# Splitting a kernel's first loads by need and over two queues, with the first projections ahead of the folded weights

## The reference, cut to what matters

```python
k = conv1x1(xA, wk, bk)         # all three: 256 channels -> 128, n = 1024 places
v = conv1x1(xA, wv, bv)
q = conv1x1(xA, wq, bq)
attn = softmax(einsum('bcn,bcm->bnm', v, q), axis=2)
av   = einsum('bcn,bnm->bcm', k, attn)
avw  = einsum('oc,bcn->bon', wwg, av)
avw  = (avw - bn1_m) * bn1_g / sqrt(bn1_v + eps) + bn1_b
o    = conv1x1(avw, wout, bout)
o    = (o - bn2_m) * bn2_g / sqrt(bn2_v + eps) + bn2_b
x    = relu(o + xA)
# then, per image: t = t + attention(layernorm(t)); t = t + experts(layernorm(t))
```

## Time and profile before

| | us |
|---|---|
| median of 3 runs | 1248.38 |
| lowest and highest | 1245.92, 1252.49 |
| the profiled execution | 1251.72 |
| its span, first to last instruction | 1249.9 |
| PE busy in it | 1120.8 (90%) |
| DVE busy | 794.2 (64%) |
| ACT busy | 634.3 (51%) |
| POOL busy | 577.8 (46%) |

### The profile page before, as it was taken

One profiled execution on the slowest core, in us unless ns is written; L12 is line 12 of the kernel. 1 busy time (PEld: TensorE's weight loads), 2 busy tenths in 40 slices (PEclk: granted clock), 3 DMA queues, 4 the chain that ended last, 5 costly groups with the idle time before them and its releaser, 6 DMA issues.

```text
span 1249.9 us, 28738 instructions
## 1 busy us (share of the span) xinstructions
PE 1120.8 (90%) x10344; PEld 739.8 (59%) x10344; DVE 794.2 (64%) x1458; ACT 634.3 (51%) x1147; POOL 577.8 (46%) x461
## 2 busy tenths in 40 slices
PE   3999999975799999899989998689899999999993
PEld 1555555533344554454445444578799989998772
DVE  2666666655788888678768872666566555555540
ACT  0757575742477668666765675433233333333432
POOL 2425242413488761675276337256454444454420
PEclk9999999977799999999999999799999999999996
DMA  5235852544022230333243214623333233332228
GB/s 164 63 114 185 317 187 80 186 130 146 27 74 78 83 78 27 96 95 95 63 109 88 57 45 127 251 36 71 51 50 47 47 49 51 53 52 40 41 31 273
DMA packets 98854, 120.50 MB, mean 96 GB/s; under 512 B 29120, under 2 KB 76032, under 8 KB 98080
## 3 DMA queue, kind: packets, MB, share of 16 engines
q1 hardware_dynamic: 77744, 70.15, 19.0%
q0 software_dynamic: 20544, 42.22, 15.2%
q10 hardware_dynamic: 432, 6.29, 1.3%
HBM read 72.84 MB, written 45.60 MB: 95 GB/s over the span
## 4 chain that ended last, share of the span: by engine, by line
PE 80%; DVE 5%; DMA 4%; ACT 3%; issue 3%; SPq 1%; DVEq 1%; another core or an unknown queue 0%; POOL 0%; ACTq 0%; POOLq 0%
PE PP L945 25%; PE PP L1313 14%; PE PP L1201 9%; PE PP L1175 9%; PE PP L1029 4%; PE PP L1080 4%; PE PP L1126 3%; PE PP L1185 3%; PE PP L1190 2%; DVE mxp L1539 2%; PE PP L977 2%; DMA WB<-late_d 2%; ACT WB L872 1%; PE PP L1054 1%; PE PP L1280 1%
## 5 line engine op out<-in xcount | busy, mean ns | idle before, releaser
L872 ACT ACTIVATE WB<-PP 128x512 f32<-128x512 f32 x512 | 268.4, 604 | 174.8 <-PE PP L1201 174.8
L1539 DVE TENSOR_REDUCE mxp<-PP 128x2 f32<-128x1024 f32 x256 | 301.3, 1219 | 66.0 <-PE PP L1126 64.4
L916 ACT ACTIVATE WORK<-PP,b1c 128x256 f32<-128x256 f32 (+1 forms) x320 | 142.4, 450 | 266.0 <-PE PP L945 248.5
L945 PE MATMUL PP<-WORK,WB 128*128 128x256 f16 (+2 forms) x1984 | 221.1, 268 | 18.1 <-issue 9.7
L672 POOL TENSOR_TENSOR WB<-WB 128x1024 f32<-128x1024 f32 x80 | 188.9, 2361 | 78.2 <-PE PP L1190 69.4
L945 PEld LDWEIGHTS PP<-WORK,WB 128*128 (+1 forms) x1984 | 186.1, 103 | 49.2 <-issue 21.4
L728 POOL DMA_INDIRECT res_d<-WORK,lb x71 | 116.1, 1635 | 200.1 <-DVE WORK L1779 180.2
L1313 PE MATMUL PP<-WB,WORK 128*128 x1704 | 194.9, 273 | 0.0
L1313 PEld LDWEIGHTS PP<-WB,WORK 128*128 128x128 f16 x1704 | 164.4, 98 | 22.0 <-issue 0.9
L1201 PE MATMUL PP<-WORK 97*128 97x256 f16 x1024 | 159.3, 279 | 16.0 <-ACT WB L872 12.9
L638 POOL TENSOR_TENSOR WB<-WORK,WB 128x1024 f16<-128x1024 f32 x32 | 68.4, 2137 | 174.0 <-ACT WORK L778 173.9
(11 more groups left out here) (287 smaller groups left out, 1144.0 us busy)
## 6 DMA issues: line engine op xcount, KB each, us to landing
WORK<-in_L_ffn_W_dram POOLq DMA_DIRECT2D x32, 512.0 KB, 4.3
res_d<-WORK SPq DMA_DIRECT2D x8, 1024.0 KB, 4.5
late_d<-WB POOLq DMA_DIRECT2D x1, 6144.0 KB, 19.1
WB<-late_d ACTq DMA_DIRECT2D x3, 2048.0 KB, 14.8
v_d<-WORK SPq DMA_DIRECT2D x4, 1024.0 KB, 4.5
WORK<-q_hi_d SPq DMA_DIRECT2D x16, 256.0 KB, 3.6
WORK<-v_d SPq DMA_DIRECT2D x8, 512.0 KB, 5.8
WORK<-k_hi_d SPq DMA_DIRECT2D x16, 256.0 KB, 3.9
```

What stands on the lines that cost most here:

```text
L872: act.activation(PR[n % 3][:, c // 2, c % 2 * 2:c % 2 * 2 + 2], SCORES[m % 3] .rearrange("p (h n) -> p h n", h=2), ACT.Exp).then_inc(s("e_ ...
L916: act.activation(hid[:, k, 0:width], hidden_bank(k)[:, 0:width], ACT.Gelu, bias=b1c[:, bass.ds(e, 1), k], scale=1.0 / WSCALE)\
L945: mm = pe.matmul(dst, lhsT, rhs, start=(n == 0), stop=(n == len(pairs) - 1))
L1539: dve.tensor_reduce(mxp[:, n // 4 % 2, i, h:h + 2, k], PP[2 + h // 2][:, :].rearrange("p (h n) -> p h n", h=2), X_AXIS, ALU.max).then_inc( ...
```

## The change

The list of 28 loads is taken apart. SyncE issues `wq` and `wv` first, on a semaphore of their own (`ld_qv`), then the first image, then the other seven weights on `ld_w`, and raises the 27 semaphores of `PLACES` only then. The vectors go to ScalarE's queue, at the head of its program, as 13 loads on `ld_vec`: where a vector has 256 values, one load fills two columns of `vec`, where there were two loads. TensorE transposes `wq` and `wv` as soon as these two are there, each into the PSUM tile that has no other use then, and VectorE copies them one by one (`wqv_kept`). TensorE projects q, waits for the seven weights, transposes the remaining ones, projects v, computes the folded weights, and projects k. `dve_prep` counts three steps now: the constants' input (1), the copies of the remaining transposes (2), the folded weights (3). Nothing is computed otherwise than before.

```diff
-LOADS = 28
+LOADS = 7
+VECTORS = 13
@@ sync
-            for name in PLACES.split():
-                sp.sem_inc(s(name), FREE)
+            sp.dma_start(wq_raw, wq).then_inc(s("ld_qv"), 16)
+            sp.dma_start(wv_raw, wv).then_inc(s("ld_qv"), 16)
+            load_x(0)
             n_w = 0
-            for dst, src in ((wq_raw, wq), (wv_raw, wv), (wk_raw, wk),
+            for dst, src in ((wk_raw, wk),
                              (wo_raw, wout.rearrange("(c p) i -> p c i", p=P)), (wwg_raw, wwg),
...
-                             (vec[:, BQ:BQ + 1], col(bq)), (vec[:, BV:BV + 1], col(bv)),
...
+            for name in PLACES.split():
+                sp.sem_inc(s(name), FREE)
...
-            load_x(0)
             load_x(1)
@@ scalar
+            for at, src in ((BQ, bq), (BV, bv), (BK, bk), (G1, bn1_g), (BB1, bn1_b), (M1, bn1_m), (V1, bn1_v),
+                            (BO, bout), (G2, bn2_g), (BB2, bn2_b), (M2, bn2_m), (V2, bn2_v), (BA, b_out)):
+                n = src.shape[0] // P
+                act.dma_start(vec[:, at:at + n], src.rearrange("(c p) -> p c", p=P), allow_slow_non_contiguous=True).then_inc(s("ld_vec"), 16)
             act.wait_ge(s("dve_prep"), 1)
             act.activation(vec[:, 24:27], vec[:, 24:27], ACT.Sqrt).then_inc(s("act_prep"), 1)
-            act.wait_ge(s("dve_prep"), 2)
+            act.wait_ge(s("ld_vec"), 16 * VECTORS)
@@ tensor
             pe.wait_ge(s("pool_const"), 1)
-            pe.wait_ge(s("ld_w"), 16 * LOADS)
...
+            pe.wait_ge(s("ld_qv"), 32)
+            for i, raw in enumerate((wq_raw, wv_raw)):
+                for c in range(CC):
+                    mm = pe.transpose(PP[3 - i][:, 2 * i * C + c * P:2 * i * C + (c + 1) * P],
+                                      raw[:, c * P:(c + 1) * P], identf[:, :])
+                mm.then_inc(s("pe_prep"), 1)
...
+            pe.wait_ge(s("wqv_kept"), 1)
             for c in range(CC):
                 project_q(0, c)
+            pe.wait_ge(s("ld_w"), 16 * LOADS)
+            for c in range(CC):
+                pe.transpose(PP[2][:, c * P:(c + 1) * P], wo_raw[:, c], identf[:, :])
+            pe.transpose(PP[2][:, 384:384 + E * HC], b1_raw, identf[0:E * HC, 0:E * HC])
+            pe.transpose(PP[2][:, 256:384], wwg_raw, identf[:, :]).then_inc(s("pe_prep"), 1)
+            pe.wait_ge(s("wqv_kept"), 2)
             project_v(0)
+            pe.wait_ge(s("dve_prep"), 2)
+            for c in range(CC):
+                product(PP[3][:, 512 + c * P:512 + (c + 1) * P], [(wk_raw[:, c * P:(c + 1) * P], wwgT)])
+            pe.wait_ge(s("ones_kept"), 1)
+            product(PP[3][:, 896:896 + E], [(ones_all, wr_raw[:, c]) for c in range(CC)])
+            product(PP[3][:, 768:896], [(bkr, wwgT)], "pe_prep")
+            pe.wait_ge(s("dve_prep"), 3)
             project_k(0)
@@ vector
-            dve.wait_ge(s("ld_w"), 16 * LOADS)
...
+            for i, dst in enumerate((wqT, wvT)):
+                dve.wait_ge(s("pe_prep"), i + 1)
+                dve.tensor_copy(dst, PP[3 - i][:, 2 * i * C:(2 * i + 1) * C].rearrange("p (c n) -> p c n", c=CC))\
+                   .then_inc(s("wqv_kept"), 1)
+            dve.wait_ge(s("ld_vec"), 16 * VECTORS)
...
+            dve.sem_inc(s("dve_prep"), 1)
+            dve.wait_ge(s("pe_prep"), 3)
+            dve.tensor_copy(woT, PP[2][:, 0:256].rearrange("p (c n) -> p c n", c=CC))
+            dve.tensor_copy(wwgT, PP[2][:, 256:384])
+            dve.tensor_copy(b1c[:, :, :], PP[2][:, 384:384 + E * HC].rearrange("p (e k) -> p e k", e=E))
```

More of the change, by code:

```diff
@@ L325, in s @@
             return S[name]
-        for name in ("q_low v_low ld_w ld_x0 ld_x1 ld_y0 ld_y1 bst_kept pool_const pe_prep dve_prep act_prep "
+        for name in ("ld_qv ld_vec wqv_kept q_low v_low ld_w ld_x0 ld_x1 ld_y0 ld_y1 bst_kept pool_const pe_prep dve_prep act_prep "
                      "q_made v_made k_made q_kept v_kept k_kept sc_made max_kept exp_kept ks_kept "
@@ L373, in _ @@
             assert n_w == LOADS
-            xv = x.rearrange("b (c p) h w -> b p c (h w)", p=P)
+            for name in PLACES.split():
+                sp.sem_inc(s(name), FREE)
             qk_d = ((q_hi_d, q_lo_d), (k_hi_d, k_lo_d))
-            def load_x(n):
-                for c in range(CC):
-                    sp.dma_start(XB[n][:, c], xv[n:n + 1, :, c, :].rearrange("o p n -> p (o n)"))\
-                      .then_inc(s(f"ld_{'xy'[n % 2]}{c}"), 16)
             def load_m(b, g, par):
@@ L1366, in per_expert @@
                 return a.unsqueeze(1).broadcast_to((P, n, E))
[L1369 removed]
             dve.memset(ones_all, 1.0).then_inc(s("ones_kept"), 1)
[L1371 to L1376 removed]
+            dve.memset(held16[:, :], 0.0)
+            for i, dst in enumerate((wqT, wvT)):
[3 more added lines that the diff above has]
+            dve.wait_ge(s("ld_vec"), 16 * VECTORS)
             dve.tensor_scalar(bkr, identf[:, :], 0.0, vec[:, BK:BK + 1], ALU.mult, ALU.add)
```

52 lines of the change are left out of this document (14 added, 38 removed).

## The result

| | before | after |
|---|---|---|
| median, us (runs) | 1250.49 (14) | 1242.57 (14) |
| lowest and highest | 1245.92, 1255.46 | 1237.96, 1247.19 |
| the profiled execution | 1251.72 | 1245.98 |
| its span | 1249.9 | 1244.2 |
| start of the first maximum | 39.81 | 34.11 |

The ratio is 0.9941 with a 95% interval of 0.9924 to 0.9957: the change makes the kernel 7.4 us faster, 5.4 to 9.5. The forecast was 1239.9 us, 8.5 us faster, in a range of 1232 to 1247. In the two profiled executions the mark moved by 5.70 us and the span by 5.7.

A forecast was written before the change was run, and what follows sets the result against it. Load issuing and waiting until 18.1 us, then TensorE's chain, were taken to bound the start; 15.2 + 8.4 + 7.7 = 31.3 us against 39.81 saves 8.5 us: 1248.38 - 8.5 = 1239.9 us, range 1232 to 1247.

The forecast's parts named there:

- the mark: VectorE's start of the first maximum, 39.81 us before; forecast at 31.3 us, bounds 27.4 to 37.9 us.
- The sum: Start of the kernel: T, then 8.4 us, then 7.7 us give the mark at 31.3 us, 8.5 us saved.
- That the mark carries the whole gain: Behind the mark the same distances as before: its shift and the span's agree within a few microseconds.
- T: Landing of all seven weights, awaited before the remaining transposes and v; forecast 15.2 us, bounds 13.1 to 17.6 us.
- q: TensorE's q projection beside the weights' landing: begins at 6 us, takes 5.2 us if four instructions are slow, bounds 3.4 to 6.9.
- V: Landing of the vectors from ScalarE's queue: about 13 us, before T, with about 5 us of cover before the folded weights.
- v: TensorE's v projection after T and four transposes: 5.2 us with four slow instructions again, bounds 3.4 to 6.9 us.
- From the folded weights' copies to the mark: Keys, VectorE's low halves, first scores: 3.6 + 2.6 + 1.5 = 7.7 us, where 14.1 us passed before; VectorE late.
- st_zero: Wait on GpSimd's table store, issued at 12.76 us before, perhaps 16 us after; about 4 us to land, hidden by 11 us.
- Part of it only: Rival at the kernel's start: T nearer 17.6 us, TensorE slow throughout; 2 to 6 us saved, about 1244.5 us; 20%.
- Slower: Rival: column loads on ScalarE's queue land late, delaying folded weights; V decides from T + 5 us; 1255 us; 6%.
- More: Rival at the start: vectors fit into transfer gaps, TensorE quick; 11 to 12.4 us saved, about 1236.5 us; 12%.

The follow-up runs named there:

- e5: Changed kernel with GpSimd's table store and first two loads (experts' weights) issued only once the seven weights have landed; 1237.92 us, ratio 0.9911 to before.
- e6: Changed kernel plus two matmuls with unread results behind q and two behind k, keeping TensorE busy; 1241.98 us, ratio 0.9948 to before.
- e3: Changed kernel with the vectors back on SyncE's queue as nineteen loads, behind the seven weights and ahead of the second image; 1238.31 us, ratio 0.9909 to before.
- e4: Changed kernel with vectors loaded as 19 rows of 128 values on ScalarE's queue, turned by one TensorE transpose; 1240.30 us, ratio 0.9932 to before.
- e9: Changed kernel with vector rows, experts' weights, table store and second image late, w_qkv split off VectorE, spare matmuls ahead of and behind q; 1235.63 us, ratio 0.9888.
- e8: e4 with the second image issued only once the seven weights have landed; 1239.29 us, ratio 0.9916 to before.
- e10: Changed kernel with all thirteen vector loads issued twice on ScalarE's queue, first into a tile nobody reads; 1243.00 us, ratio 0.9949 to before.
- e7: Changed kernel with the split of w_qkv moved from VectorE to ScalarE and GpSimd; 1240.57 us, ratio 0.9925 to before.
- e2: New TensorE and VectorE order, but all loads on SyncE's queue as in the kernel before; 1247.89 us, ratio 0.9987 to before.

## Why the prediction was right, and where it was off

**The sum.** It put the mark at 15.2 + 8.4 + 7.7 = 31.3 us, 8.5 us sooner. The first profile has 17.0 + 8.9 + 8.2 = 34.1 us, and the three together a mean mark of 33.05 us, 6.8 us sooner. The median fell by 7.4 us, so the forecast saving of 8.5 us missed the median's by 1.1 us and that of the first profile's mark by 2.8 us. Most of the latter miss is T. The forecast time, 1239.9 us, is 2.7 us below the measured one; 2.1 us of this are that the three runs of before that I had counted from lay below its later median (1248.38 and 1250.49 us).

**That the mark carries the whole gain: right.** Over the changed kernel and the ten experiments, y1 came sooner by 85.6 us in sum, and the medians by about 90. Single kernels stray from their y1 by up to 3.5 us (e5 has 13.1 us at y1 and 11.1 in the median, e6 10.0 and 6.5), so this holds for the sum, and for the order only roughly. A point much further back agrees: ScalarE's first transfer of `late_d`, behind the attention (L893 before, at 775.9 us; L895 after, at 769.5 us), comes sooner in all thirteen profiles, by 1.2 to 3.8 us more than y1. Nothing that was gained at the start had been lost by then.

**T, said 15.2 us:** 17.0 in the first profile, 15.5 to 16.1 in five others. The form of the term was right (bytes in front, plus what the vectors take), its size 0.3 to 1.8 us short. Within it, e3 shows that the vectors beside the weights cost 1.7 to 3.2 us, around the 2.1 I took, but the working of the 2.1 was wrong, and that it came near is luck. I had divided the shares by the two loads that are issued in a microsecond. What the engines moved in the one from 12 us was 593 packets, more than four loads of 128 values have; a price for each packet gives 1.1 to 1.3 us for all 2432 values (below), and T = 14.4 us at most. The rest of the cost is not the engines' time for the values. A part of it is that `b1` was issued later than I had it: in the changed kernel SyncE's issues take longer than before. SyncE's queue after:

```profile
4.92 0.98 SPq L372 DMA_DIRECT2D WORK<-in_L_ffn_Wr_dram  x1
...
6.62 0.57 SPq L372 DMA_DIRECT2D WORK<-in_L_ffn_b_dram  x1
```

The same queue with the vectors behind the weights (e3):

```profile
4.71 0.47 SPq L372 DMA_DIRECT2D WORK<-in_L_ffn_Wr_dram  x1
...
5.80 0.58 SPq L372 DMA_DIRECT2D WORK<-in_L_ffn_b_dram  x1
```

`b1` is issued 0.8 us later in the first. In the eight profiles with single values on ScalarE's queue it is issued at 6.2 to 6.6 us, in e3 at 5.80. That both queues issue is not enough: with rows on ScalarE's queue it was 5.74 us in e4 and e9, but 6.51 in e8. What makes the issues slow isn't shown.

**q, said from 6 us for 5.2 us:** from 6.75 us for 6.45. It was slow in full, and within the bound of 6.9; it had cover enough, since TensorE waited 3.8 us behind it. It cost nothing. Only e9, with work from 1.07 us on, had it quick.

**V, said 13 us with 5 us of cover: wrong by 7 us.** ScalarE's queue after:

```profile
0.76 0.41 ACTq L756 DMA_DIRECT2D vec<-in_L_conv_bq_dram  x1
...
8.08 2.91 ACTq L756 DMA_DIRECT2D vec<-in_L_attn_b_out_dram  x1
```

The thirteen issues took 10.2 us, not 5.9, the last of them alone 2.91 us, and its load landed 12.0 us after its issue where I had let it take 6.0. I had the price of an issue from a queue that issued alone, and that of the landing from the kernel before, where the transfer engines were full for a shorter time. e5 shows how much of it was the load on them: with GpSimd's loads held back the last issue took 0.57 us and V was 15.4. Of the cover, counted from T, 2.3 us were left in the first profile, so the miss didn't reach the end. In e3, e6 and e10, where the path in front was shorter or V later, it did (in e6 by about 0.1 us). The rival's rule, that V decides from T + 5 us, holds only with a slow v: V - T was 3.1 us after, with 2.3 us to spare, which is T + 5.4. With a quick v the point is T + 3: e3 had a V - T of 4.4 us and waited 1.48 us, e6 had 3.0 and hardly waited.

**v, said 5.2 us:** 5.8 (5.3 and 5.9 in the two others), because the pause before it let the clock fall. It was quick behind pauses of 0.5 to 2.1 us (e3, e5, e6, e8) and behind none (e9), and slow behind those of 2.3 to 3.8 us (e10, e7, e4 and all three profiles of the changed kernel). The rule that I weighed in the prediction, that of the Trainium skill ("TensorE: Matmul & The Clock Gate", What's actually happening), had v and the folded weights slow. The rows take a middle course: v slow in most of its instructions, the folded weights quick (1.28 us).

**From the folded weights' copies to the mark, said 7.7 us:** 8.2. VectorE is late, as I had it, and e7 shows it. What I had not let happen is a second fall of the clock, behind a pause of only 1.93 us: all three profiles of the changed kernel and e4 show it. In e2, e3, e5, e8 and e10 the same pause left the scores quick. In four of these five v was quick before; in e10 v was slow and the scores were not, so what v did isn't the whole of it, and what decides stays open.

**The table's store, `st_zero`: hidden,** as said. GpSimd issued it at 16.88 us, 17 us ahead of the mark.

**The rivals.** "Part of it only" described what the first profile shows (T at 17.0 us, TensorE slow), and its 2 to 6 us meet that profile's 5.7; but the median's 7.4 us lies in the forecast's own 6 to 11, though its interval (5.4 to 9.5) reaches into both. "Slower" had its mechanism present and its price far from enough: e10 put twice the loads there and stayed faster. "More" is what e3 and e5 reach, by moving vectors or bytes out of the way.

## What to carry to other kernels

Put the loads in the order in which the engines need them, count every byte that stands in front of the one that ends a wait, whoever issues it, and hold back bulk that is used late: that brought the mark to 26.71 us, where the changed kernel's three profiles have 31.82 to 34.11. Here small loads of single values were better behind the weights than beside them on a second queue (1238.31 against 1242.57 us), and a price read from a queue that ran alone is too low for one that shares its engines. An early load gained little here until the program was ready for it (2.9 us), and the program's new order little without the load (1.6 us, not told from nothing); and where a wait of some us goes, look whether the clock falls in what is left of it.

## What the runs showed of the hardware

- Loads of 128 single values are dear in engines, not in bytes. Before, between 12 and 14 us, the queue moved 1415 packets at a share of 37% of sixteen engines: 0.37 x 2 x 16 / 1415 = 8 ns of one engine for each, an estimate. The transfers of this stretch (queue, packets, MB, share):

```profile
q1 hardware_dynamic: 1415, 0.01, 37.0%
```

  At that price 2432 values are 1.3 us of all engines; at that of the microsecond from 16 us (399 packets at 18.8%) they are 1.1 us. e3's gain in T is larger, so this is not all of it.
- An issue on a queue of SyncE or ScalarE took 0.41 to 0.46 us at first and up to 1.13 us later in the three profiles of the changed kernel, and the thirteenth of ScalarE 2.91, 3.15 and 2.91 us. That long one is 2.7 to 3.3 us in every profile with single values on ScalarE's queue, but for e5, where GpSimd's loads are held back: 0.57 us. With SyncE alone (e3) an issue took 0.40 to 0.62 us, once 1.17 us, and one of a row on ScalarE's queue (e4) 0.24 to 0.53 us.
- The column of the granted clock reads 1.00 while q goes at the slow pace from 6.75 us on (6.45 us, against 3.67 in e9). It tells when the clock falls, not that TensorE has reached its pace at the start.
- An operation of GpSimd held up a copy of VectorE. VectorE's timeline of e9, where GpSimd's subtraction ran from 16.57 to 19.67 us:

```profile
17.85 1.98 DVE L1425 COPY idw<-identf 128x256 f32<-128x256 f32 x1
19.75 0.16 DVE L1426 TENSOR_TENSOR idw<-WORK,wmean 128x16 f32<-128x16 f32 x1
```

  The copy took 0.29 us in every kernel without that subtraction, and ends here only after the subtraction has ended; in e7 it took 1.45 us and ended at 26.33 us, with the subtraction's end at 26.18. The three operations on PSUM just ahead of it were not held up. The Trainium skill ("SBUF — State Buffer", SBUF: two separate sides) says that GpSimd and such copies of VectorE lock one pair of ports for a whole instruction; both traces agree.
